# All four down products ahead of the adapter's product, the second sample's residual behind it in transposing mode, and the last expert sums in transposing mode

## The chip, the cores and the metric

The kernel runs on one core of a Trainium2 chip. A core has a matrix engine (TensorE, PE in the rows; its weight loads are PEld), VectorE (DVE), ScalarE (ACT), GpSimd (POOL), SyncE (SP), and 16 DMA engines. The metric is the device time of one launch in microseconds; the median of the runs stands for a kernel. Each engine works through its own list of instructions in order, and waits on semaphores that others raise.

## What is computed

Two layers over x of shape (4, 256, 128): an adapter whose 32x32 matrix is picked by a domain number, then layer norm; then a style-modulated mixture of 8 experts, of which each token takes two.

```python
# layer 0, the adapter (A = 32, 16 domains)
hidden = gelu(x @ down_W.T + down_b, approximate=False)
hidden = hidden @ expert_W[idx].T + expert_b[idx]      # hidden itself where the domain is invalid
hidden = hidden + domain_emb[idx]
x1 = layernorm(hidden @ up_W.T + up_b + x) * ln_gamma + ln_beta
# layer 1
h = (layernorm(x1) * ln_g + ln_b), normalised again over the 256 tokens of a sample
gamma, beta = split(style network of the subject)      # softplus on gamma
h = h_norm * gamma + beta
gates, idx = top_k(softmax(h @ router_w), 2)           # divided by their sum
eout_e = relu(h @ exp_w1[e] + exp_b1[e]) @ exp_w2[e] + exp_b2[e]
out = x1 + sum over e of gate_e * eout_e
```

## The kernel before

The 4 samples of 256 tokens are called b = 0 to 3; the first half is samples 0 and 1, the second half 2 and 3. A sample is T = 2 tiles of 128 tokens. x comes in transposed (features on partitions) as `xT_sb`, in two transfers: samples 0 and 1 on SP's queue, samples 2 and 3 on ACT's queue as its third transfer (semaphore `x_loaded[1]`). The order on every engine is written out by hand.

**The front.** VectorE makes `w_diag` (lines 781 to 808), the picked expert matrices laid out for the four samples, from the domain numbers and the tables. TensorE multiplies it by the up matrix (line 654, "the adapter's product", four matmuls into bank 4), and VectorE adds the bias to give `up_eff` (line 819): picked expert and up matrix in one. `down(b)` (line 559) is x times the down matrix of sample b, into bank 2 for samples 0 and 1 and bank 3 for samples 2 and 3; `down(2)` waits for `x_loaded[1]`. ScalarE takes each through gelu into `hidden` (line 444), in the order of b, and then loads another activation table (line 446) for the logarithms and exponentials that make every reciprocal root (lines 453 and 455). `residual(b)` (line 565) writes x of the sample, turned back to tokens on partitions, into its sum bank, as two matmuls with the identity. `up(b)` (line 573) adds hidden times `up_eff` on top of it in the same bank and so waits for gelu of b, for `up_eff`, and for the residual ahead of it. VectorE then takes the sum's statistics (line 876), aggregates them (line 888), centres (line 905), writes x1 (line 913), takes its statistics and normalises, and TensorE transposes the result (line 583) for the second normalisation, which makes `h_high` and `h_low`.

**The experts.** 8 experts by 2 halves give 16 blocks of 4 units; for each unit TensorE runs three matmuls of 512 columns for the first product (lines 594, 595, 613) and three for the second (594, 595, 633), ScalarE rounds the relu (508) and writes it in full (511), and VectorE subtracts for the low part (1005, or 1008 and 1010). The second product of a unit runs three units behind its first product.

**The end.** The last block belongs to the second half. The sum of the others stands transposed in `y_sum`. TensorE transposes the first half's (line 743, four matmuls called with the transposing mode). For the second half it writes `y_sum` turned into the two banks `sum_last` (line 750: four ordinary matmuls with the identity, `start` at the first of each bank) and adds the last block's `y_part` (line 756: four more), each sample's pair of 756 waiting for VectorE's piece of `y_part` (line 1161, two pieces). VectorE adds x1 for each of the four samples (line 1165), and SP stores the output in three transfers (line 293): both samples of the first half, then sample 2, then sample 3.

Of the kernel before, what the change touches and what calls it, by code (L numbers as in the profile page):

```python
# [99 lines left out]
def adapter_moe(nc, xT, ids, tables, early, style, ln_row, w_all, out):  # L100
    ctx = ExitStack()
    with ctx:
# [195 lines left out]
        def _(pool):  # L298
# [74 lines left out]
            def load_high(e):  # L373

                if e >= W_RING:
                    pool.wait_ge(down_done, FC * (1 + max(k for k, (i, _) in enumerate(BLOCKS) if i == e - W_RING)))
                pool.dma_start(w_high[:, e % W_RING, :], w_all[:, e, :]).then_inc(w_high_loaded[e], 16)  # L377
# [173 lines left out]
        def _(pe):  # L551
            mm = nc.tensor.matmul

            def down(b):

                if b % HB == 0:
                    pe.wait_ge(x_loaded[b // HB], 16)
                row = (b % HB) * SLOT
                mm(down_ps[b // HB][row:row + A, 0:S], EARLY.of(early_sb, "down"), xT_sb[:, b * S:(b + 1) * S],
                   start=True, stop=True, tile_position=(0, row)).then_inc(down_in_psum, 1)  # L560

            def residual(b):

                for t in range(T):
                    mm(sum_ps[b][:, t, :], xT_sb[:, (b * T + t) * P:(b * T + t + 1) * P], ident[:, :],
                       start=(t == 0), stop=False, skip_group_check=True)

            def up(b):

# [73 lines left out]
            pe.wait_ge(ident_ready, 1)  # L643
            pe.wait_ge(x_loaded[0], 16)
            residual(0)
            pe.wait_ge(early_loaded, 16)
            down(0)
            down(1)
            residual(1)
            pe.wait_ge(w_diag_ready, 1)  # L650
            for b in range(B):

# [3 lines left out]
                          skip_group_check=True)  # L656
            last.then_inc(up_eff_in_psum, 1)

            down(2)
            down(3)  # L660
            pe.wait_ge(ones_ready, HB)
            pe.wait_ge(up_eff_ready, 1)
            up(0)
# [2 lines left out]
            pe.wait_ge(onehots_ready, 1)  # L666
            mm(se_ps, STYLE.of(style_sb, "subj", SUBJ), onehot_s[:, :], start=True, stop=True).then_inc(style_in_psum, 1)
            residual(2)
            pe.wait_ge(style_ready, 1)
            mm(hyp1_ps, STYLE.of(style_sb, "hyp1", SE), se_T[:, :], start=True, stop=True).then_inc(style_in_psum, 1)  # L670
# [76 lines left out]
            for b in range(HB, B):  # L747
                for t in range(T):
                    j = (b - HB) * T + t
                    mm(sum_last[b - HB][:, t * P:(t + 1) * P], y_sum[:, 1, j * P:(j + 1) * P], ident[:, :],  # L750
                       start=(t == 0), stop=False, skip_group_check=True)
            for b in range(HB, B):
                pe.wait_ge(y_taken, N_BLOCKS - 1 + b - HB + 1)
                for t in range(T):
                    j = (b - HB) * T + t
                    last = mm(sum_last[b - HB][:, t * P:(t + 1) * P], y_part[:, 1, j * P:(j + 1) * P], ident[:, :],
                              start=False, stop=True, skip_group_check=True)
                last.then_inc(yT_in_psum, 1)


# [473 lines left out]
```

## Time and profile before

| | us |
|---|---|
| median of 3 runs | 119.65 (119.27 to 119.68) |
| the profiled execution, its own time | 119.94 |
| its span, first to last instruction | 118.2 |
| TensorE busy | 112.0 |
| VectorE busy | 91.8 |
| ScalarE busy | 84.3 |
| GpSimd busy | 54.1 |

The profile shows one execution. Its own time is 1.74 us more than its span, which is what lies around the instructions, and it is 0.29 us above the median of the runs. A timeline row gives start and duration in us, the engine, the line, what is written and read, how many instructions are merged (x4), and in brackets how long the engine stood before it and what ended that. A matmul of fp32 operands appears as two passes, so the two matmuls of a residual are x4 in a row; the four transposes of line 743 appear as x4, one pass each. Passes overlap: from one start to the next is less than the duration of one.

### The profile page before, as it was taken

What the parts mean: (1) busy time and instruction counts of PE and PEld (TensorE: products, weight loads), DVE (VectorE), ACT (ScalarE), POOL (GpSimd) and SP (SyncE); (2) the same over time, 40 slices, a digit from 0 to 9 for tenths busy, and PEclk for the clock granted to TensorE, in tenths of its full rate; (3) what the DMA queues carried; (4) which work ended last, traced back from release to release, by engine and by line L of the source; (5) the groups of instructions that cost most, each with busy time, mean ns of one, the idle gap of its engine ahead of it and who ended that gap; (6) DMA issues with size and microseconds to landing.
All of it is one profiled execution on the core that took longest, in us unless ns stands there. A gap on an engine that the chain in (4) does not pass through costs nothing.

```text
span 118.2 us, 1665 instructions
## 1 busy us (share of the span) xinstructions
PE 112.0 (95%) x519; PEld 84.3 (71%) x519; DVE 91.8 (78%) x228; ACT 84.3 (71%) x153; POOL 54.1 (46%) x75
## 2 busy tenths in 40 slices
PE   6799988999999999999999999999999999999990
PEld 2157534777777888688888888888888888888780
DVE  4486988999899989997685959595867777776772
ACT  2139845698999988697878787878778687878400
POOL 5020889226417000101259999976758941322310
PEclk9999999999999999999999999999999999999999
DMA  4939699994000000326999300000000000000005
GB/s 68 343 97 365 173 374 442 384 412 150 0 0 3 0 6 0 89 100 165 415 446 408 169 0 6 0 0 0 0 0 0 0 0 0 6 0 0 0 0 178
DMA packets 4473, 14.17 MB, mean 120 GB/s; under 512 B 561, under 2 KB 1905, under 8 KB 4209
## 3 DMA queue, kind: packets, MB, share of 16 engines
q1 hardware_dynamic: 3024, 9.67, 21.9%
q0 software_dynamic: 1008, 3.67, 8.8%
q10 hardware_dynamic: 432, 0.73, 2.2%
q8 instruction: 4, 0.07, 0.2%
q14 instruction: 5, 0.03, 0.1%
HBM read 13.52 MB, written 0.56 MB: 119 GB/s over the span
## 4 chain that ended last, share of the span: by engine, by line
PE 72%; DVE 14%; ACT 5%; issue 3%; DMA 3%; POOL 1%; DVEq 0%; ACTq 0%; POOLq 0%
PE bank L594 22%; PE bank L595 22%; PE bank L633 12%; PE bank L613 11%; DMA ids_i<-ids_dram 3%; DVE x L913 2%; ACT hid_high L508 2%; DVE stats L920 1%; ACT bank L511 1%; DVE hid_low L1005 1%; DVE bank L905 1%; POOL z L370 1%; PE bank L750 1%; DVE stats L876 1%; PE bank L583 1%
## 5 line engine op out<-in xcount | busy, mean ns | idle before, releaser
L508 ACT ACTIVATE hid_high<-bank,early_sb 128x512 fp32r<-128x512 f32 x64 | 44.2, 691 | 15.9 <-PE bank L613 15.8
L1005 DVE TENSOR_TENSOR hid_low<-bank,hid_high 128x512 fp32r<-128x512 f32 x51 | 34.8, 687 | 16.7 <-ACT bank L511 16.1
L511 ACT ACTIVATE bank<-bank,early_sb 128x512 f32<-128x512 f32 x51 | 33.6, 658 | 0.0
L308 POOL TENSOR_TENSOR w_low<-w_raw,w_high 128x256 fp32r<-128x256 f32 x32 | 22.7, 734 | 12.3 <-DMA w_high<-w_all_dram 4.4
L633 PE MATMUL bank<-hid_low,w_high 128*128 128x512 f32 x64 | 25.9, 405 | 0.4 <-DVE hid_low L1010 0.2
L594 PE MATMUL bank<-h_high,w_low 128*128 128x512 f32 x64 | 25.5, 398 | 0.3 <-ACT h_high L486 0.3
L594 PE MATMUL bank<-hid_high,w_low 128*128 128x512 f32 x64 | 25.6, 400 | 0.0
L595 PE MATMUL bank<-h_high,w_high 128*128 128x512 f32 x64 | 25.3, 396 | 0.0
L613 PE MATMUL bank<-h_low,w_high 128*128 128x512 f32 x64 | 25.1, 397 | 0.0
L595 PE MATMUL bank<-hid_high,w_high 128*128 128x512 f32 x64 | 25.0, 390 | 0.0
L318 POOL TENSOR_TENSOR y_sum<-y_sum,y_part 128x512 f32<-128x512 f32 x9 | 11.6, 1292 | 17.3 <-DVE y_part L1025 15.1
L633 PEld LDWEIGHTS bank<-hid_low,w_high 128*128 128x128 f32 x64 | 12.0, 187 | 5.5 <-DVE hid_low L1005 2.1
L594 PEld LDWEIGHTS bank<-hid_high,w_low 128*128 128x128 f32 x64 | 12.0, 188 | 3.0
L613 PEld LDWEIGHTS bank<-h_low,w_high 128*128 128x128 f32 x64 | 12.0, 188 | 3.0 <-DVE h_low L994 0.2
L594 PEld LDWEIGHTS bank<-h_high,w_low 128*128 128x128 f32 x64 | 12.0, 188 | 2.9 <-ACT h_high L486 0.6
L595 PEld LDWEIGHTS bank<-h_high,w_high 128*128 128x128 f32 x64 | 12.0, 188 | 2.7
L595 PEld LDWEIGHTS bank<-hid_high,w_high 128*128 128x128 f32 x64 | 12.1, 188 | 2.7
L377 POOL DMA_DIRECT2D w_high<-w_all_dram x7 | 4.1, 581 | 21.0 <-PE bank L633 15.4
L638 PE MATMUL bank<-busy 128*128 128x512 bf16 (+1 forms) x30 | 9.0, 438 | 1.2 <-DVE busy L770 1.1
L1008 DVE TENSOR_SCALAR bank<-bank,early_sb 128x512 f32<-128x512 f32 x13 | 9.7, 749 | 0.0
L1010 DVE TENSOR_TENSOR hid_low<-bank,hid_high 128x512 fp32r<-128x512 f32 x13 | 9.0, 691 | 0.4
L1025 DVE SCALAR_TENSOR_TENSOR y_part<-bank,early_sb,gate_all 128x512 f32<-128x512 f32 x9 | 6.7, 742 | 0.0
(136 smaller groups left out, 99.2 us busy)
## 6 DMA issues: line engine op xcount, KB each, us to landing
w_high<-w_all_dram POOLq DMA_DIRECT2D x7, 512.0 KB, 7.9
w_raw<-w_all_dram SPq DMA_DIRECT2D x1, 2560.0 KB, 10.9
gate_all<-gate_scratch SPq DMA_DIRECT2D x4, 512.0 KB, 5.9
gate_all<-gate_scratch SPq DMA_DIRECT2D x1, 2048.0 KB, 12.5
w_raw<-w_all_dram SPq DMA_DIRECT2D x3, 512.0 KB, 3.9
style_sb<-style_dram SPq DMA_DIRECT2D x1, 324.0 KB, 5.6
tables_sb<-tables_dram ACTq DMA_DIRECT2D x1, 272.0 KB, 3.8
xT_sb<-xT_dram SPq DMA_DIRECT2D x1, 256.0 KB, 4.4
```

The costliest lines, as they stand in the source:

```text
L308: nc.gpsimd.tensor_tensor(w_low[:, e % W_RING, quarter(q)], w_raw[:, e, quarter(q)], w_high[:, e % W_RING, quarter(q)].bitcast(F32), ALU.s ...
L318: nc.gpsimd.tensor_tensor(y_sum[:, h, :], y_sum[:, h, :], y_part[:, h, :], ALU.add).then_inc(y_added, 1)
L508: ac(hid_high[:, slot, :], hid_ps[slot][:, :], ACT.Relu, bias=bias).then_inc(relu_steps, 1)
L511: ac(hid_ps[slot][:, :], hid_ps[slot][:, :], ACT.Relu, bias=bias).then_inc(relu_steps, 1)
L594: mm(ps, w_low[:, e % W_RING, w], moving_high, start=first, stop=False)
L595: mm(ps, w_high[:, e % W_RING, w], moving_high, start=False, stop=False)
L613: mm(hid_ps[q % RING][:, :], w_high[:, e % W_RING, c * P:(c + 1) * P], half_of(h_low, h), start=False, stop=True).then_inc(hid_in_psum, 1)
L633: mm(ps, w_high[:, e % W_RING, w], hid_low[:, slot, :], start=False, stop=c == FC - 1).then_inc(down_done, 1)
L638: mm(ps[:, 0:columns], busy[:, :], busy[:, :].unsqueeze(1).broadcast_to([P, columns // P, P]), start=True, stop=True)
L1005: v.tensor_tensor(low, ps, high.bitcast(F32), ALU.subtract).then_inc(low_vector, 1)
L1008: v.tensor_scalar(ps, ps, col(b1_col(q)), 0.0, ALU.add, ALU.max).then_inc(vector_relu, 1)
L1010: v.tensor_tensor(low, ps, high.bitcast(F32), ALU.subtract).then_inc(low_vector, 1)
```

## The change

On TensorE alone, in three places:

- `down(2)` and `down(3)` go ahead of the adapter's product, directly behind `down(0)` and `down(1)`. With them the wait for `x_loaded[1]` goes ahead of it.
- `residual(1)` goes behind the adapter's product, and its two matmuls are called with `is_transpose=True`.
- The eight matmuls of lines 750 and 756 are called with `is_transpose=True`. Their order, their banks and their waits stay.

```diff
             down(0)
             down(1)
-            residual(1)
+            down(2)
+            down(3)
             pe.wait_ge(w_diag_ready, 1)
             for b in range(B):
...
             last.then_inc(up_eff_in_psum, 1)
 
-            down(2)
-            down(3)
+            residual(1, one_pass=True)
             pe.wait_ge(ones_ready, HB)
             pe.wait_ge(up_eff_ready, 1)
             up(0)
...
                     mm(sum_last[b - HB][:, t * P:(t + 1) * P], y_sum[:, 1, j * P:(j + 1) * P], ident[:, :],
-                       start=(t == 0), stop=False, skip_group_check=True)
+                       is_transpose=True, start=(t == 0), stop=False, skip_group_check=True)
...
                     last = mm(sum_last[b - HB][:, t * P:(t + 1) * P], y_part[:, 1, j * P:(j + 1) * P], ident[:, :],
-                              start=False, stop=True, skip_group_check=True)
+                              is_transpose=True, start=False, stop=True, skip_group_check=True)
```

In `residual` the new argument is passed on to the matmul; it is `False` for samples 0, 2 and 3.

The first place is on TensorE, from the down products of samples 0 and 1 (line 559, bank 2) to the first up product (line 573). Bank 3 takes the down products of samples 2 and 3, bank 4 the adapter's product (line 654 before, 655 now), bank 1 the residual of sample 1 (line 565).

```order
 L559 MATMUL bank2<-xT_sb,early_sb 32x256 [waits x_loaded0,early_loaded]
 L559 MATMUL bank2<-xT_sb,early_sb 32x256
-L565 MATMUL bank1<-ident,xT_sb 128x128 x2
-L654 MATMUL bank4<-early_sb,w_diag 64x128 [waits w_diag_ready]
-L654 MATMUL bank4<-early_sb,w_diag 64x128 x3
 L559 MATMUL bank3<-xT_sb,early_sb 32x256 [waits x_loaded1]
 L559 MATMUL bank3<-xT_sb,early_sb 32x256
+L655 MATMUL bank4<-early_sb,w_diag 64x128 [waits w_diag_ready]
+L655 MATMUL bank4<-early_sb,w_diag 64x128 x3
+L565 MATMUL bank1<-ident,xT_sb 128x128 x2
 L573 MATMUL bank0<-up_eff,hidden 128x128 [waits gelu_ready,up_eff_ready,ones_ready]
 L573 MATMUL bank0<-up_eff,hidden 128x128
```

The adapter's product moved behind the instruction that waits for the second transfer of x, and the residual moved behind the adapter's product.

The second place is the end of TensorE's list, from the last product of the last expert (line 633, bank 5). These rows are of the changed kernel; the kernel before has the same ones, word for word.

```order
L633 MATMUL bank5<-hid_low,w_high 128x512 [waits low_vector]
L743 MATMUL bank6<-ident,y_sum 128x128 [waits y_added,gates_T_ready]
L743 MATMUL bank6<-ident,y_sum 128x128 x3
L750 MATMUL bank7<-ident,y_sum 128x128 [waits first_added]
L750 MATMUL bank7<-ident,y_sum 128x128
L750 MATMUL bank0<-ident,y_sum 128x128 x2
L756 MATMUL bank7<-ident,y_part 128x128 [waits y_taken]
L756 MATMUL bank7<-ident,y_part 128x128
L756 MATMUL bank0<-ident,y_part 128x128 [waits y_taken]
L756 MATMUL bank0<-ident,y_part 128x128
```

Nothing moved there: only the mode of lines 750 and 756 differs. A row counts matmuls, not passes. VectorE, ScalarE, GpSimd and SP have the same rows as before throughout.

## Rows read from the trace of the kernel before

**Rows 1.** The page: shares of the chain that ended last, by engine.

```profile
PE 72%; DVE 14%; ACT 5%; issue 3%; DMA 3%; POOL 1%; DVEq 0%; ACTq 0%; POOLq 0%
```

**Rows 2.** Waits from 19 to 113 us: total, times, longest.

```profile
PEld bank L633 <- DVE hid_low L1005: 2.1, 6, 0.5
```

**Rows 3.** Timeline of TensorE's matmuls, 5.8 to 9.7 us.

```profile
5.80 0.68 PE L565 MATMUL bank<-ident,xT_sb 128*128 128x128 f32 x4 [0.72 <-DMA xT_sb<-xT_dram]
6.42 0.63 PE L559 MATMUL bank<-xT_sb,early_sb 128*32 128x256 f32 x4
6.97 0.71 PE L565 MATMUL bank<-ident,xT_sb 128*128 128x128 f32 x4
7.75 0.66 PE L654 MATMUL bank<-early_sb,w_diag 128*64 128x128 f32 x8
8.34 0.63 PE L559 MATMUL bank<-xT_sb,early_sb 128*32 128x256 f32 x4
8.98 0.72 PE L573 MATMUL bank<-up_eff,hidden 33*128 33x128 f32 x8
```

**Rows 4.** Timeline of VectorE, 7.3 to 12.6 us.

```profile
7.39 0.30 DVE L808 TENSOR_TENSOR w_diag<-w_eff,in_sample 128x132 f32<-128x132 f32 x1
...
8.45 0.42 DVE L819 TENSOR_TENSOR up_eff<-bank,early_sb 128x256 f32<-128x256 f32 x1
9.70 0.89 DVE L876 BATCH_NORM_STATS2 stats<-bank 128x6 f32<-128x128 f32 x4 [0.82 <-PE bank L573]
...
12.02 0.60 DVE L913 SCALAR_TENSOR_TENSOR x<-bank,rstd,ln_sb 128x128 f32<-128x128 f32 x2
```

**Rows 5.** Both transfers of x: issue rows, then KB and us to landing.

```profile
1.25 0.42 SPq L270 DMA_DIRECT2D xT_sb<-xT_dram  x1
...
1.73 0.46 ACTq L438 DMA_DIRECT2D xT_sb<-xT_dram  x1
...
xT_sb<-xT_dram SPq DMA_DIRECT2D x1, 256.0 KB, 4.4
xT_sb<-xT_dram ACTq DMA_DIRECT2D x1, 256.0 KB, 5.8
```

**Rows 6.** Timeline of ScalarE, 8.9 to 11.6 us.

```profile
8.99 0.95 ACT L444 ACTIVATE hidden<-bank,early_sb 32x256 f32<-32x256 f32 x2 [0.90 <-PE bank L559]
9.96 1.28 ACT L446 ACT_TABLE_LOAD   x1
11.26 0.30 ACT L453 ACTIVATE log_var<-mv,eps 128x4 f32<-128x4 f32 x1
```

**Rows 7.** Timeline of TensorE's matmuls, the end.

```profile
113.01 0.60 PE L743 MATMUL bank<-ident,y_sum 128*128 128x128 f32 x4
113.44 1.06 PE L750 MATMUL bank<-ident,y_sum 128*128 128x128 f32 x8
114.33 1.06 PE L756 MATMUL bank<-ident,y_part 128*128 128x128 f32 x8
```

**Rows 8.** Timeline of VectorE and SP's queue at the end; the stores' landing.

```profile
113.20 0.88 DVE L1161 SCALAR_TENSOR_TENSOR y_part<-bank,early_sb,gate_all 128x256 f32<-128x256 f32 x2 [0.59 <-PE bank L633]
114.00 0.74 DVE L1165 TENSOR_TENSOR z<-bank,x 128x256 f32<-128x256 f32 x2
114.77 0.39 SPq L293 DMA_DIRECT2D out_dram<-z  x1
...
114.98 0.87 DVE L1165 TENSOR_TENSOR z<-bank,x 128x256 f32<-128x256 f32 x2 [0.24 <-PE bank L756]
115.43 0.94 SPq L293 DMA_DIRECT2D out_dram<-z  x2
...
out_dram<-z SPq DMA_DIRECT2D x2, 128.0 KB, 1.9
```

**Rows 9.** Stretches: each engine's busy us (instructions); TensorE's granted clock; DMA.

```profile
5.08:5.80 0.72, 0.00 (x1) 0.03 (x1) 0.72 (x2) 0.00 (x0) 0.00 (x0) 1.00 0.99 382
...
112.50:115.90 3.40, 2.72 (x21) 2.46 (x21) 2.50 (x7) 0.00 (x0) 0.09 (x1) 1.00 0.05 16
```

More of the change, by code:

```diff
@@ L560, in down, with residual @@
                    start=True, stop=True, tile_position=(0, row)).then_inc(down_in_psum, 1)
-            def residual(b):
+            def residual(b, one_pass=False):
                 for t in range(T):
                     mm(sum_ps[b][:, t, :], xT_sb[:, (b * T + t) * P:(b * T + t + 1) * P], ident[:, :],
-                       start=(t == 0), stop=False, skip_group_check=True)
+                       is_transpose=one_pass, start=(t == 0), stop=False, skip_group_check=True)
             def up(b):
@@ L750, in _ @@
                     mm(sum_last[b - HB][:, t * P:(t + 1) * P], y_sum[:, 1, j * P:(j + 1) * P], ident[:, :],
-                       start=(t == 0), stop=False, skip_group_check=True)
+                       is_transpose=True, start=(t == 0), stop=False, skip_group_check=True)
             for b in range(HB, B):
```

## The prediction

> **What bounds the kernel now.** I read the chain that ended last first: 72% of it is TensorE, 14% VectorE [rows 1]. Then the waits in the long expert stretch: TensorE's weight loads wait there for VectorE's `hid_low`, six times, 2.1 us in all [rows 2], and for no DMA. So from 19.7 us on the kernel is a stretch of TensorE work whose length doesn't depend on when it starts, and two places are left where the change can act: the front, which sets when it starts, and the tail behind the last product. The two timelines of the front [rows 3, 4] show its chain: `w_diag` ends at 7.69, the adapter's product starts at 7.75, `up_eff` runs 8.45 to 8.87, `up` starts at 8.98, and VectorE, which stood 0.82 us for it, then goes from 9.70 through the first layer norm. The thing to see is that `residual(1)` (6.97 to 7.68) fills the time before `w_diag` and `down(2)`, `down(3)` (8.34 to 8.97) fill the time in which VectorE makes `up_eff`. Both stand under a cover already. In the tail [rows 7, 8] VectorE stands 0.24 us for line 756 and SP's last store is issued right behind the last sum.
>
> **Part 1: down products ahead of the adapter's.** What they now wait for is the second transfer of x. It is issued at 1.73 and lands 5.8 us later, at 7.53; the first one, 1.25 + 4.4, lands at 5.65, and TensorE's first pass on it starts at 5.80, 0.15 later [rows 3, 5]. The cheapest reaction between engines is the 0.06 from `w_diag` to line 654 [rows 3, 4]. So `down(2)` starts between 7.59 and 7.68; I take the middle, 7.63. Two down products take 0.55 us from start to next start at 6.42 and 0.64 at 8.34, where the next one waited too [rows 3]; I take 0.59. The adapter's product, queued behind them, then starts at 8.22 in place of 7.75: 0.47 later. `w_diag` is ready at 7.69, as before, and no longer the last to come. `up_eff` follows by the same amount. In the kernel before, the up product had 0.05 us of slack behind it (8.87 + 0.06 = 8.93 against a start at 8.98, since `down(3)` was still going through), and that slack is free now: **0.42 us later**, with ends of 7.59 + 0.55 - 7.75 - 0.05 = 0.34 and 7.68 + 0.64 - 7.75 - 0.05 = 0.52.
>
> Who waits for that: everything behind the first up product on TensorE, so VectorE's statistics at 9.70, and VectorE is nearly without a gap from there to the x1 of sample 0 at 12.02 [rows 4]. The first normalisation, `h_high` and the first expert product come later by the same 0.42.
>
> **What the earlier down products give.** Gelu of samples 2 and 3 started at 8.99 after 0.90 us of standing for line 559; they took 0.95, the table load 1.28, and the first logarithm started at 11.26, where the table was in [rows 6]. With `down(2)` at 7.63 in place of 8.34 this chain can be some 0.7 us earlier. That is the gain one would look for, and I book it at nothing: the logarithm also needs the aggregated statistics of VectorE, which follow `up`. The root takes 0.30 and a shorter exponential, so it was there before 11.9, and `x1` at 12.02 started because VectorE came free from the work before it, not because the root arrived. With VectorE 0.42 later the table is out of the way with time to spare, and what is late next is VectorE. The cover that makes it worth nothing is VectorE's own row of work; if it weren't there, the gain would be at most 11.26 less the old time of the statistics, some 0.3 us.
>
> **Part 2: `residual(1)` in one pass, behind the adapter's product.** Before: four passes in 0.71 us ahead of 7.75, hidden by the wait for `w_diag`. Now two passes, and they run while VectorE makes `up_eff` (0.42 us and two reactions of 0.06). The four passes of line 743 are 0.43 us from start to the next line's start, 0.11 a pass [rows 7], so two are 0.22 and fit. Cost nothing, gain nothing. Without that cover they would cost 0.22. TensorE stands from about 7.0 to 7.63; a stand of 0.72 us at 5.08 to 5.80 went by with the granted clock at 1.00 [rows 9], that is at 2.4 GHz, so I book no clock.
>
> **Part 3: the last sums in one pass.** Lines 750 and 756 were eight passes each, 0.89 us from 113.44 to 114.33; line 743, which is the same shape in transposing mode, has one pass a matmul at 0.11 [rows 7]. So 750 is 0.44 instead of 0.89 and ends its issue at 113.88. Line 756 for sample 2 needs the first piece of `y_part`, one half of the 0.88 from 113.20, so 113.66, and starts at 113.88; its two passes end by 113.99 + 0.27 = 114.3. Sample 3's piece is there at 114.08, its sum at 114.5. VectorE is busy with the sums of samples 0 and 1 until 114.74 [rows 8]: both are ready before it asks. Its 0.24 us of standing goes, and the other two sums run at the pace of the first two, 0.33 a piece (0.74 less one duration of 0.41): the last ends at 114.00 + 3 x 0.33 + 0.41 = 115.40 instead of 115.85. What is late next is SP: its first store is issued at 114.77 for 0.39, and the other two take 0.94 together. They can start at 115.21 (0.05 between issues) instead of 115.43: **0.22 us earlier**. Ends: 0.45 if the issues shrink as VectorE's end moves, and nothing if the last store's landing (1.9 us from its issue [rows 8]) is held up by the ones before it. I take 0.22, as SP's issues are the row nearest to it.
>
> Here a rule speaks against the change. The granted clock was 1.00 through 112.5 to 115.9, with four transposing passes among the ordinary ones [rows 9]. The Trainium skill, "TensorE: Matmul & The Clock Gate", Part 4: PE-mode transpose, says that the full clock doesn't engage for transposing mode, because it doesn't count as busy in the same way. By that, twelve transposing passes in a row could run at 1.2 GHz.
>
> **The sum.** +0.42 at the front, -0.22 at the end: +0.20. The profiled execution, 119.94, would be 120.14; from the median, 119.65 + 0.20 = 119.85. Within 0.5% (0.6 us) is about what a measurement of this kernel can't tell from no change.
>
> **Rivals.**
> 1. *The second transfer of x lands late* (slower). The front's end follows the landing one for one, which it did not before, when `down(2)` came at 8.34. Landing at 7.53 gives +0.20; beyond 7.93 the sum is over +0.6, and at 8.3, the last moment at which the old order would not have felt it, it is +0.97: 120.6. For it: it is the third transfer on its queue and took 1.4 us longer than the first half [rows 5]. Against: three runs within 0.4 us speak for steady transfers. Chance 13%.
> 2. *It lands by 7.1.* Then the down products fit ahead of `w_diag`, the loss is nil or a slack of 0.05, and the tail's gain stays: 119.4. For it: the profile itself adds records, and its run is 0.29 above the median. Chance 14%.
> 3. *The edit doesn't bring one pass.* Accumulating in transposing mode may still be issued as two passes: no gain at the tail, 119.65 + 0.42 = 120.07. Against: lines 743 and 565 write the same shapes, one and two passes [rows 3, 7]. 4%.
> 4. *The clock falls in the tail.* Then a pass is at most twice 0.11, eight are as long as the sixteen were, and the gain goes: 120.07. That is the result the skill's sentence would give; the row shows 1.00 so far. 2%.
> 5. *The waits in the expert stretch shift.* The 2.1 us of [rows 2] are small coincidences of ScalarE and VectorE at the seam between the halves. With ScalarE's gelu and table load earlier and VectorE later these meet differently. Losing 0.8 of them would make it 119.0 (7%), adding 0.5 would make it 120.35 (5%).
>
> **The numbers.** Forecast 55%, rivals as above. Faster by over 0.5%: 7% from rival 5 and 1% of rival 2, 8%. Slower: 13% of rival 1 and 5% of rival 5, 18%. Within: 74%. The range takes in rival 2 and the upper ends of the two terms (+0.52 with no gain at the tail, 120.17) and a part of rival 5: 119.2 to 120.3.
>
> **What would show it.** Right: TensorE standing from about 7.0 until the landing of the second transfer, line 655 near 8.2, `up_eff` near 8.9, VectorE's statistics near 10.1, gelu of samples 2 and 3 done by 9.1, the first expert product 0.4 later; at the end eight passes fewer, no wait of VectorE for line 756, the last sum 1.4 us behind the start of the first one, three store issues back to back. Wrong: statistics still at 9.7 (an early landing), x1 moving by less than the statistics (then the table load had been on the path), or sixteen passes at the end.

## The result, and the profile after

| | before | after |
|---|---|---|
| median of 22 runs each, us | 119.39 | 120.03 |
| ratio after to before, 95% interval | | 1.0045 (1.0027 to 1.0062) |
| profiled execution, own time and span, us | 119.94, 118.2 | 120.00, 118.2 |

The changed kernel is slower by 0.45%, 0.54 us, where 0.20 was forecast. It is within the stated range, and on the edge of what the 0.5% bound calls no change. Here and below a median is of all runs, while a ratio leaves out the few slow executions in which the granted clock fell (one of 125.52 us at 0.945 here); so the medians differ by 0.64. The two profiles show next to nothing of it: their spans are equal. The profile of the kernel before is the odd one: its own time, 119.94, is above every run of that kernel that the ratios here and below count (118.74 to 119.83), while 120.00 is an ordinary time of the changed kernel. So the first question is what the pair of profiles hides.

The timeline of TensorE after, the front (answers to [rows 3]):

```profile
4.92 1.19 PE L565 MATMUL bank<-ident,xT_sb 128*128 128x128 f32 x4
6.04 0.92 PE L559 MATMUL bank<-xT_sb,early_sb 128*32 128x256 f32 x4
7.57 0.63 PE L559 MATMUL bank<-xT_sb,early_sb 128*32 128x256 f32 x4 [0.60 <-DMA xT_sb<-xT_dram]
8.12 0.66 PE L655 MATMUL bank<-early_sb,w_diag 128*64 128x128 f32 x8
8.71 0.44 PE L565 MATMUL bank<-ident,xT_sb 128*128 128x128 f32 x2
9.35 0.72 PE L573 MATMUL bank<-up_eff,hidden 33*128 33x128 f32 x8 [0.20 <-issue]
```

VectorE after (answers to [rows 4], with the stand of line 836, of which more below):

```profile
6.59 0.30 DVE L808 TENSOR_TENSOR w_diag<-w_eff,in_sample 128x132 f32<-128x132 f32 x1
...
8.83 0.42 DVE L819 TENSOR_TENSOR up_eff<-bank,early_sb 128x256 f32<-128x256 f32 x1 [1.32 <-PE bank L655]
10.07 0.89 DVE L876 BATCH_NORM_STATS2 stats<-bank 128x6 f32<-128x128 f32 x4 [0.82 <-PE bank L573]
...
14.85 0.34 DVE L836 SCALAR_TENSOR_TENSOR soft<-gamma_raw 128x4 f32<-128x4 f32 x1
```

TensorE stands 0.60 us for the second transfer of x, which landed at the same moment as before (1.72 + 5.8). The adapter's product starts at 8.12, and `up` at 9.35: 0.37 later than in [rows 3], against 0.42 forecast. But `w_diag` was ready at 6.89 here and at 7.69 before. In this execution the domain numbers had landed 0.8 us earlier, and VectorE stood 1.32 us for the adapter's product. The first half of x was early too: it landed at 4.75 (1.25 + 3.5) here, at 5.65 before, and at 4.2 to 5.0 in every other profile. The old order would have used a part of that, down to where its own `residual(1)` ends; the new one can't use any of it.

ScalarE after (answers to [rows 6]): gelu and the table load come 0.77 earlier, and then the engine stands for VectorE, as the prediction said.

```profile
8.22 0.95 ACT L444 ACTIVATE hidden<-bank,early_sb 32x256 f32<-32x256 f32 x2 [0.21 <-PE bank L559]
9.19 1.28 ACT L446 ACT_TABLE_LOAD   x1
11.39 0.30 ACT L453 ACTIVATE log_var<-mv,eps 128x4 f32<-128x4 f32 x1 [0.92 <-DVE mv L888]
```

The first expert product, after, and then before (a row that wasn't shown ahead):

```profile
19.81 0.47 PE L594 MATMUL bank<-h_high,w_low 128*128 128x512 f32 x1 [0.30 <-ACT h_high L486]
```

```profile
19.66 0.47 PE L594 MATMUL bank<-h_high,w_low 128*128 128x512 f32 x1 [0.30 <-ACT h_high L486]
```

That is 0.15 later, not 0.37: 0.22 us of the loss is made up between the statistics and here. The waits in the expert stretch are those of [rows 2] to the digit:

```profile
PEld bank L633 <- DVE hid_low L1005: 2.1, 6, 0.5
```

The tail after (answers to [rows 7, 8]):

```profile
113.57 0.60 PE L750 MATMUL bank<-ident,y_sum 128*128 128x128 f32 x4
...
114.01 0.69 PE L756 MATMUL bank<-ident,y_part 128*128 128x128 f32 x4
...
114.13 1.41 DVE L1165 TENSOR_TENSOR z<-bank,x 128x256 f32<-128x256 f32 x4
114.90 1.50 SPq L293 DMA_DIRECT2D out_dram<-z  x3
```

Each matmul takes one pass, VectorE's four sums run in one row without a stand (1.41 from the start of the first to the end of the last, 1.40 forecast), and the three stores take 1.50 us where they took 1.60 before.

### The profile page after: what moved, and what is told of

It is laid out like the page before. It is cut to its first block, busy times and chain, and to the rows that moved or that the text cites. A ratio compares the mean times of both kernels' runs of the same rounds, so it can differ in the third digit from the quotient of the medians.

```text
span 118.2 us, 1645 instructions
## 1 busy us (share of the span) xinstructions
PE 111.5 (94%) x509; PEld 83.4 (71%) x509; DVE 91.4 (77%) x228; ACT 84.3 (71%) x153; POOL 54.2 (46%) x75
## 4 chain that ended last, share of the span: by engine, by line
PE 74%; DVE 11%; DMA 5%; ACT 3%; issue 3%; POOL 1%; ACTq 1%; DVEq 0%; POOLq 0%
PE bank L594 23%; PE bank L595 23%; PE bank L633 12%; PE bank L613 12%; DMA xT_sb<-xT_dram 5%; DVE x L913 2%; ACT hid_high L508 1%; DVE stats L920 1%; DVE bank L905 1%; ACT bank L511 1%; DVE z L1165 1%; POOL z L370 1%; DVE stats L876 1%; DVE y_part L1161 1%; PE bank L583 1%
```

## The experiments

**Theory A**: the loss is the adapter's product waiting for x's second transfer; the tail gives a little back. **Rivals**: B, the tail's gain is nil; C, the loss comes from `residual(1)` moved or in its new mode. All ratios are to the kernel before, run beside each on the same chip. The rows stand in three groups of four, each group measured together on one chip, so small ratios compare best inside a group.

| run | median us | ratio | interval |
|---|---|---|---|
| tail alone | 119.03 | 0.9998 | 0.9975 to 1.0021 |
| front alone | 119.60 | 1.0032 | 1.0005 to 1.006 |
| adapter's product first | 119.11 | 0.999 | 0.9969 to 1.0012 |
| x's second half early | 119.01 | 0.998 | 0.9959 to 1.0001 |
| GpSimd, first edit | 119.44 | 1.0019 | 1.0001 to 1.0037 |
| adapter first + GpSimd | 119.51 | 1.002 | 1.0001 to 1.0039 |
| the same + x early | 119.46 | 1.0012 | 0.9993 to 1.0032 |
| down products alone | 120.29 | 1.0067 | 1.0043 to 1.0092 |
| GpSimd, second edit | 118.72 | 0.9964 | 0.9942 to 0.9986 |
| all together | 118.75 | 0.9957 | 0.9936 to 0.9978 |
| domain numbers late, before | 120.29 | 1.0082 | 1.0057 to 1.0107 |
| domain numbers late, changed | 120.19 | 1.0069 | 1.0043 to 1.0095 |

**1. Down products alone.** The kernel before with one edit:

```diff
             residual(1)
+            down(2)
+            down(3)
             pe.wait_ge(w_diag_ready, 1)
...
             last.then_inc(up_eff_in_psum, 1)
-            down(2)
-            down(3)
             pe.wait_ge(ones_ready, HB)
```

> The kernel before with nothing but down(2) and down(3) put ahead of the adapter's product; residual(1) stays where it was, in two passes, and the tail too. Theory A: the whole loss of the front is here, as slow as the run of the front part, ratio 1.003 to 1.0065. Rival C (the move or the mode of residual(1) costs): about 1.000.

Measured 1.0067, just past the expected end: the loss is in this one move. Rival C falls. Its TensorE rows:

```profile
7.52 0.62 PE L559 MATMUL bank<-xT_sb,early_sb 128*32 128x256 f32 x4
8.07 0.66 PE L656 MATMUL bank<-early_sb,w_diag 128*64 128x128 f32 x8
```

The adapter's product is at 8.07 with `residual(1)` in two passes a matmul and in its old place, against 8.12 in the changed kernel, each time 0.55 behind the start of `down(2)`. Mode and place of the residual move nothing here.

**2. The front alone**, lines 750 and 756 back in ordinary mode.

> The front part of the change alone; lines 750 and 756 as before. Theory A: slower than before by 0.6 to 0.9 us (the changed kernel's 0.54 and what the tail gave), ratio 1.005 to 1.0075. Rival B: the same as the changed kernel, 1.0045.

1.0032, below the stated 1.005: a miss in size, though clearly above no change. The interval takes in both the changed kernel's ratio and the lower part of the expected ones, so this run doesn't decide on rival B.

**3. The tail alone**, on the kernel before:

```diff
                     mm(sum_last[b - HB][:, t * P:(t + 1) * P], y_sum[:, 1, j * P:(j + 1) * P], ident[:, :],
-                       start=(t == 0), stop=False, skip_group_check=True)
+                       is_transpose=True, start=(t == 0), stop=False, skip_group_check=True)
...
                     last = mm(sum_last[b - HB][:, t * P:(t + 1) * P], y_part[:, 1, j * P:(j + 1) * P], ident[:, :],
-                              start=False, stop=True, skip_group_check=True)
+                              is_transpose=True, start=False, stop=True, skip_group_check=True)
```

> Lines 750 and 756 in transposing mode, nothing else. Theory A (the change loses at the front, where the adapter's product now waits for the second transfer of x, and gains a little at the tail): 0.1 to 0.3 us faster than before, ratio 0.9975 to 0.999, and eight passes fewer behind line 743. Rival B (the tail is held by the stores' landing, so one pass gives nothing): ratio 1.000.

0.9998 is outside what was expected, and its interval takes in both theories: the ratio can't tell 0.1 us from nothing. The profiles can, from the start of line 1161 to the span's end, since nothing ahead of it matters there. With two passes a matmul: before 5.00 (118.2 less 113.20), and 4.95 to 4.99 in the other five profiles. With one: after 4.86, and 4.87 to 4.93 in the other seven. That is about 0.1 us, and it is in SP's row of stores: 1.60 or 1.61 in all six, 1.49 or 1.50 in all eight. Rival B is wrong, but so was the 0.22 of the forecast.

**4. The adapter's product first.** The changed kernel with this:

```diff
             down(1)
-            down(2)
-            down(3)
             pe.wait_ge(w_diag_ready, 1)
...
             residual(1, one_pass=True)
+            down(2)
+            down(3)
```

> The changed kernel with down(2) and down(3) put back behind the adapter's product and the one-pass residual(1). Theory A: the wait for the second transfer of x is out of the adapter's way, so the product starts with w_diag (7.75 or, in an execution in which the domain numbers land early, 6.95): 0.2 to 0.6 us faster than before, ratio 0.995 to 0.998. Rival C (the loss comes from residual(1) moved behind the adapter's product or from its mode): as slow as the changed kernel, 1.0045.

0.999 (0.9969 to 1.0012) misses the expected 0.995 to 0.998: the loss is gone, the gain beyond that isn't shown. TensorE, and a row of VectorE to which experiment 8 comes back:

```profile
6.65 0.66 PE L653 MATMUL bank<-early_sb,w_diag 128*64 128x128 f32 x8
7.24 0.44 PE L565 MATMUL bank<-ident,xT_sb 128*128 128x128 f32 x2
7.61 0.63 PE L559 MATMUL bank<-xT_sb,early_sb 128*32 128x256 f32 x4
8.16 0.72 PE L573 MATMUL bank<-up_eff,hidden 33*128 33x128 f32 x8
...
13.69 0.63 DVE L836 SCALAR_TENSOR_TENSOR soft<-gamma_raw 128x4 f32<-128x4 f32 x1
```

The product is 1.47 us earlier than in the changed kernel, `up` 1.19 earlier. `up` now stands behind `down(2)` and `down(3)`, as in the kernel before; that is why it gains less than the product did. The old order has the same bound where the numbers are early: in the profile of the tail alone `down(2)` starts at 7.43, when the second transfer of x lands (1.73 + 5.7), and `up` at 7.98. So putting the adapter's product first gives nothing over the kernel before in such an execution.

**5. x's second half early.** The changed kernel, its order kept, with the transfers behind x's first half on SP's queue held back, the style weights and the layer norm row first among them:

```diff
+            sp.wait_ge(x_loaded[0], 16)
             sp.dma_start(style_sb[:, :], style).then_inc(style_loaded, 16)
```

> The changed kernel with the transfers of the style weights and of the layer norm row held back until the first half of x has landed, so that the second half of x lands sooner. Theory A: the adapter's product moves with that landing one for one; if it lands at 6.6 to 7.0 the product starts at 7.2 to 7.6 and the kernel is 0.4 to 0.7 us faster than the changed one, about equal to before. Rival C: no faster than the changed kernel.

0.998. The second half landed 4.0 us after its issue instead of 5.8; down products and adapter's product follow at once:

```profile
6.13 1.06 PE L560 MATMUL bank<-xT_sb,early_sb 128*32 128x256 f32 x8
7.12 0.66 PE L656 MATMUL bank<-early_sb,w_diag 128*64 128x128 f32 x8
```

The product is 1.00 us earlier than 8.12. The landing moved by 1.8 us (to 5.73), but TensorE's own row, `residual(0)` and the first down products, lasted until 6.13 and past it. Theory A holds from this side too: same order, no loss once the transfer is there.

**6 and 7. Late domain numbers.** In both kernels the transfer of the domain numbers goes second on its queue:

```diff
-            sp.dma_start(ids_i[:, :], ids).then_inc(ids_loaded, 16)
             sp.dma_start(xT_sb[:, 0:HN], xT[:, 0:HN]).then_inc(x_loaded[0], 16)
+            sp.dma_start(ids_i[:, :], ids).then_inc(ids_loaded, 16)
```

> The kernel before with the transfer of the domain numbers issued second instead of first on its queue, so that it lands later. Theory A: the kernel before starts its adapter's product with w_diag, which follows the domain numbers, so it gets slower by what w_diag is late beyond the old end of residual(1): 0.3 to 1.0 us, ratio 1.0025 to 1.0085.

> The changed kernel with the same edit. Theory A: its adapter's product starts at about 8.1 with the landing of the second half of x, whenever the domain numbers land, so it doesn't get slower than the changed kernel by more than 0.2 us: ratio to before 1.004 to 1.0065, and the two kernels with the late domain numbers are within 0.3 us of each other. Rival C (the loss isn't this wait): it gets slower by as much as the kernel before does.

The kernel before goes to 1.0082, as expected. The changed one goes to 1.0069, a little past the stated 1.0065, and 0.16 us above its own 120.03 of another set of runs. It doesn't follow the landing, as was expected of it (that came early, and `down(2)` started at 7.29): each kernel starts its adapter's product 0.06 behind `w_diag` now, the kernel before first, then the changed one:

```profile
8.18 0.66 PE L654 MATMUL bank<-early_sb,w_diag 128*64 128x128 f32 x8 [1.37 <-DVE w_diag L808]
```

```profile
8.03 0.66 PE L655 MATMUL bank<-early_sb,w_diag 128*64 128x128 f32 x8
```

With the numbers late the two can't be told apart; with the numbers early only the old order gains, and rival C falls once more. This is what the pair of profiles hid: the one of before had them at 4.3 us, every other profile here of a kernel that issues them first had them by 3.5 (VectorE's first operation on them started at 2.7 to 3.5).

**8. GpSimd, first edit.** Where did the 0.22 us come from that the changed kernel made up between statistics and expert product? Line 836 takes 128x4 elements and lasts 0.34 us after; before it was this, with GpSimd's splits beside it, four of 0.69 that end at 15.02 (VectorE, then GpSimd, both before):

```profile
14.47 0.57 DVE L836 SCALAR_TENSOR_TENSOR soft<-gamma_raw 128x4 f32<-128x4 f32 x1
```

```profile
12.25 2.77 POOL L308 TENSOR_TENSOR w_low<-w_raw,w_high 128x256 fp32r<-128x256 f32 x4 [3.60 <-ACT w_high L496]
```

It ends at 15.04 before and at 15.19 after, each time 0.02 behind the last split (15.02 and 15.17). With the adapter's product first it starts at 13.69 and lasts 0.63, until 14.32; the last split ends at 14.31. In the tail alone it lasts 0.14, and the operation behind it, line 927, stands in its place until 14.29; the last split ends at 14.27:

```profile
13.82 0.47 DVE L927 SCALAR_TENSOR_TENSOR z_shift<-mv,rstd 128x2 f32<-128x2 f32 x1
```

**Theory D**: VectorE stands for that split. The Trainium skill, "SBUF — State Buffer", section "Who interferes with whom", says that a VectorE instruction with two SBUF inputs contends with a GpSimd instruction that reads SBUF. Line 836 reads `gamma_raw` twice, and the trace agrees: the operation stands until the split ends. That the ports are the reason, and nothing else that the two engines share, no run here separates. **Rival E**: the operation is long of itself. On the kernel before:

```diff
-            split_lows(0)
+            split_lows(0, (0, 1, 2))
             normalise(0, T)
+            split_lows(0, (3,))
             split_lows(1, (0, 1))
```

> The kernel before, with GpSimd's first normalise put ahead of the fourth quarter of its first weight split. Theory D: VectorE's small operation of line 836 stands until GpSimd's last split of the group ends (0.57 us for 128x4 in the profile of before, 0.14 where no split was in the way), and this is where the changed kernel got 0.2 us of its loss back; with the last split out of the way line 836 or the shift behind it takes under 0.2 us and the kernel is 0.2 to 0.4 us faster than before, ratio 0.997 to 0.998. Rival E: line 836 stays long for another reason (its own operands), ratio 1.000.

Rival E falls at once, and so does the expected gain: 1.0019. VectorE, GpSimd, and TensorE's wait:

```profile
13.62 0.15 DVE L837 SCALAR_TENSOR_TENSOR soft<-gamma_raw 128x4 f32<-128x4 f32 x1
...
16.55 0.82 DVE L960 TENSOR_SCALAR t_off<-t_mv,early_sb 128x2 f32<-128x2 f32 x1
...
19.23 0.94 DVE L990 TENSOR_TENSOR h_low<-h_full,h_high 128x256 fp32r<-128x256 f32 x1
```

```profile
15.26 2.09 POOL L308 TENSOR_TENSOR w_low<-w_raw,w_high 128x256 fp32r<-128x256 f32 x3
...
18.44 1.44 POOL L308 TENSOR_TENSOR w_low<-w_raw,w_high 128x256 fp32r<-128x256 f32 x2
```

```profile
PEld bank L614 <- DVE h_low L995: 0.5, 1, 0.5
```

Line 836 (837 here) takes 0.15. But the three splits put behind the normalise end at 17.35 and line 959 (960 here, 0.29 before) at 17.37; and line 989 (990), 0.65 before, is 0.94. The stand moved to two places that are later on the path. From the statistics to the first expert product it is 10.00 us, against 9.96 before. Behind that product the lengthened line 989 costs more: TensorE's wait for `h_low` is 0.5 us where it was 0.2, and from the first expert product to the span's end it is 98.9 us, against 98.4 to 98.5 in every profile without this edit.

**9 and 10. The same edit with the adapter's product first**, without and with the style transfer held back.

> The changed kernel with the adapter's product first, as in the run of that name, and GpSimd's normalise ahead of its fourth split. Theory A with D: the two gains add, 0.3 to 0.8 us faster than before, ratio 0.9935 to 0.9975. Rival E: as the run without the GpSimd edit, 0.999.

> As the last, and the style weights' transfer held back until the first half of x has landed. Theory A: with the adapter's product first the second half of x matters only for the up product queued behind down(2) and down(3), so an earlier landing gives 0.1 to 0.3 us more: ratio 0.992 to 0.996. If the style weights or the first expert's weights then come too late, VectorE or ScalarE wait for them and the gain is gone.

1.002 and 1.0012: both miss. The edit gives nothing ahead of the first expert product (10.00 and 10.05 us from the statistics, against 10.03 with the adapter's product first alone) and costs the same 0.3 behind it (98.7 and 98.8). Holding the style transfer back gave nothing that the intervals can tell, so in experiment 5 it helped by the landing of x and not by itself.

**11. GpSimd, second edit.** All splits out of the way, on the kernel before:

```diff
-            split_lows(0)
+            split_lows(0, (0, 1, 2))
             normalise(0, T)
-            split_lows(1, (0, 1))
+            split_lows(0, (3,))
+            split_lows(1, (0,))
             load_high(2)
             load_high(3)
-            pool.wait_ge(affine_ready, HB)
-            split_lows(1, (2, 3))
+            pool.wait_ge(h_ready, 1)
+            split_lows(1, (1, 2, 3))
```

> The kernel before, with GpSimd's splits kept out of VectorE's way in the whole stretch of the second normalisation: normalise after three quarters, two quarters behind it, and the last three of expert 1 only when h_low is ready. Theory D in full (VectorE's small operations and line 989 stand until a GpSimd split ends; the first edit only moved the stand from line 836 to line 959 and lengthened the one of 989): stands of 836, 959 and 989 gone together, 0.4 to 0.7 us from the first statistics to the first expert product and its low part, ratio 0.994 to 0.997. Rival E (the first expert product is held by something else): ratio 1.000 or above.

0.9964, faster beyond its interval. All three operations are short, and between them and the first statistics lies the stretch that got shorter (VectorE, then TensorE):

```profile
9.65 0.89 DVE L877 BATCH_NORM_STATS2 stats<-bank 128x6 f32<-128x128 f32 x4 [0.82 <-PE bank L574]
...
14.42 0.15 DVE L837 SCALAR_TENSOR_TENSOR soft<-gamma_raw 128x4 f32<-128x4 f32 x1
...
17.36 0.29 DVE L960 TENSOR_SCALAR t_off<-t_mv,early_sb 128x2 f32<-128x2 f32 x1
...
19.64 0.42 DVE L990 TENSOR_TENSOR h_low<-h_full,h_high 128x256 fp32r<-128x256 f32 x1
```

```profile
19.26 0.47 PE L595 MATMUL bank<-h_high,w_low 128*128 128x512 f32 x1 [0.31 <-ACT h_high L487]
```

From statistics (9.65) to expert product (19.26) it is 9.61 us instead of 9.96, and TensorE's wait for `h_low`, 0.2 us before, isn't among its waits any more. Theory D is shown: the stands of all three lines come and go with the splits.

**12. All together**: the changed kernel with the edits of 4, 5 and 11.

> The changed kernel with the adapter's product first, the style weights' transfer held back, and GpSimd's splits as in the run before this one. If the gains add: 0.5 to 1.0 us faster than before, ratio 0.9915 to 0.996.

0.9957 (0.9936 to 0.9978), 0.5 us faster than before and inside what was expected, at its lower end. It is 9.61 us again from the statistics (8.79) to the first expert product (18.40). The changed kernel's own ratio, 1.0045, was taken in another set of runs; set against it this is some 0.9% less. Nearly all of the gain over before is the GpSimd edit's: between 11 and 12 no difference can be told.

## Why the prediction was right, and where not

- **What bounds the kernel**: right. From the first expert product to the span's end it is 98.5 us before, 98.4 after (the tail's 0.1) and 98.5 with down products alone.
- **The front, 0.42 (0.34 to 0.52)**: 0.37 in the shown pair of profiles. The start of `down(2)` (7.63 said, 7.57 seen) and the 0.59 for two down products (0.55) held. The slack of 0.05 wasn't there: product and `up` moved by the same 0.37, and `up` starts 0.10 to 0.11 behind the end of `up_eff` in both, not 0.06. The failed step is "`w_diag` is ready at 7.69, as before". It was read from one execution as if fixed, and so was the end of `residual(1)` at 7.68. In two profiles of the old order with early domain numbers the statistics start at 8.73 (tail alone, below) and 8.84 (GpSimd's first edit), against 10.02 to 10.12 in the new one (after, front alone, down products alone); in a third, GpSimd's second edit, they start at 9.65, because there `residual(1)` was late (last section). So the term is 0.4 where the numbers or the residual are late and up to 1.3 where neither is. How the timed runs divide between these can't be read, since only profiled executions show a landing; so the size of 0.54 is explained in kind and not in parts.

```profile
8.73 0.89 DVE L876 BATCH_NORM_STATS2 stats<-bank 128x6 f32<-128x128 f32 x4 [0.98 <-PE bank L573]
```

- **The rival "the second transfer lands late"** had the right place and the wrong end. The landing was steady in the profiles, 5.5 to 6.0 us from issue wherever the order of transfers was kept, but for one of 5.0; it was the other side of the comparison that moved. Its premise that the old order wouldn't feel this landing before 8.3 holds for the shown profile only: in the tail alone `down(2)` started with it, at 7.43. The opposite rival, a landing by 7.1, may have come true now and then: six of the changed kernel's 21 runs that the ratio counts took 119.0 to 119.43 us and the other fifteen 119.78 to 120.27. No profile of the changed kernel shows such a landing, so that is not shown.
- **The early table load, booked at nothing**: wrong by 0.22. The argument looked at `x1` alone, which did wait for VectorE only. The same logarithm also heads ScalarE's rounding of the first weights (line 496, 11.70 before and 11.84 after), and by it GpSimd's splits: these started at 12.25 before and 12.39 after, 0.14 later where the statistics were 0.37 later. Line 836, which ends with the splits, was therefore 0.15 later and not 0.37. That is the 0.22, given back in the changed kernel. The pair with late domain numbers shows it again: 9.97 us from the statistics to the first expert product in the old order, 9.74 in the new one. In the tail alone, with early numbers, it is 9.77, so against such executions the changed kernel gets next to nothing back.
- **`residual(1)`**: right, nothing either way.
- **The tail, 0.22**: 0.1. One pass a matmul, the vanished stand and the three stores back to back all came. The mis-sized term is "the other two take 0.94 together": back to back each issue lasted 0.51 where 0.38 and 0.49 had been taken, so half of the 0.22 was lost in SP's queue.
- **The clock in the tail**: 1.00 from 112.5 to 115.9 also after, and the passes of line 750 still 0.11 apart (0.60 less 0.27 over three). So rival 4 did not come: twelve transposing passes in a row, behind a busy stretch, ran at the full clock, against what the prediction quoted from the Trainium skill, "TensorE: Matmul & The Clock Gate", Part 4.
- **Chances**: 18% stood on slower by over 0.5%, 74% on within. 0.45% is within, by less than its interval.

In sum the sign and the chain were right, and the size held partly by luck. In the shown pair +0.37 at the front, -0.22 on the way to the first expert product and -0.1 at the tail make +0.05, and the two own times differ by 0.06. Most timed runs of the kernel before were better off than its profiled execution, and the changed kernel was not. As far as the record goes, that is where most of the 0.54 comes from, and the forecast had no term for it.

## What to carry to other kernels

Before moving work ahead of a wait, ask not when its input lands in the profile, but what the thing now queued behind it was waiting for, and how early that can be in other executions: an engine's queue makes the later of two arrivals binding for both. Where one small operation lasts several times as long as its size asks, look at which other engine's operation ends with it; and when moving that one away, check every small operation in the place where it goes.

## What the runs showed of the hardware that was not expected

A small two-input VectorE operation can last four times its length (0.57 for 0.15 us) beside GpSimd's 0.69 us splits; a scalar operation on 128x2 did the same (0.82 for 0.29, line 959), ending 0.02 behind them. And passes of the same shape took nearly twice as long in some executions up to 6 or 7 us: `residual(0)` lasted 1.19 us at 4.92 after and 0.68 at 5.80 in [rows 3], and in the run of GpSimd's second edit this went on until about 7.0, which made `residual(1)` and not `w_diag` hold the adapter's product (7.70, `w_diag` at 6.69):

```profile
4.97 1.20 PE L566 MATMUL bank<-ident,xT_sb 128*128 128x128 f32 x4
6.10 1.03 PE L560 MATMUL bank<-xT_sb,early_sb 128*32 128x256 f32 x4
```

The granted clock is given as 1.00 for that stretch too, so the records don't say why. This stays open; it may be a part of the spread of the kernel before, whose timed runs no profile covers.
